# Attention scores of two heads in the two row halves of TensorE, in an order from a model of all engines

## The chip, the cores and the metric

The kernel runs on one core of a Trainium2 chip. The metric is the device time in microseconds, the median over runs. Differences of 2% (53 us here) count as faster or slower.

## What is computed

Two transformer layers on x of shape (2, 2048, 256), with 16 heads of 16 columns each. Both feed-forward layers have weights reduced to sign and a scale. The parts around the change are the two attentions:

```python
# layer a: causal softmax, then times a decay table
att = jnp.einsum('bhqd,bhkd->bhqk', q, k) * (1.0 / math.sqrt(hd))
att = jnp.where(causal, att, -jnp.inf)
att = jax.nn.softmax(att, axis=-1)
att = att * decay_weight_matrix(T)
y = jnp.einsum('bhqk,bhkd->bhqd', att, v)
# layer b: the same without the decay, with biases on q, k, v
x = x + attention_a(layernorm(x)); x = x + ffn(layernorm(x))
x = x + layernorm_affine(attention_b(layernorm(x))); x = x + ffn(layernorm(x))
```

The decay falls to zero at a distance of about 512 positions, so of layer a only a band of keys is needed for y, while the softmax's maximum and sum need all keys.

## The kernel before

Six phases run one after the other, each with its own buffers: `setup`, `projections` (q, k and v of layer a), `attention` "att_a" (decayed), `dense` "mid", `attention` "att_b" (dense in the sense of no decay), `dense` "end". Only `attention`, the plan that orders it and a few constants of `setup` are touched.

**Operands.** q and k are kept as a high and a low part of an fp32r number. A head has 16 columns; its score is the sum of four products (high by high, high by low, and so on), laid under each other in 64 rows (`PAIRS * HD`). Rows 64 to 127 of `kop` hold ones, and row 64 (`MROW`) of `qop` holds the negated maximum of each query, so that one matmul of 128 rows gives score minus maximum. The rest of the rows in `qop` are zero. The padding is written by `pad` (L601) on VectorE and GpSimd.

**Loops.** The 2 × 16 heads are 8 groups of 4 heads (`GH`). In a group, queries come in 4 chunks of 512 (`c`), keys in 16 blocks of 128 (`kb`). The items of work are:

- M (L814 to L831): a matmul of 128 queries by up to 512 keys into one of 4 banks `pm`; VectorE reduces it to one maximum per query (L759, and L763 where the causal mask cuts it). 160 in a group.
- FX, FE, FM, FT: only in att_a, exponentials and sums of the pieces of keys beyond the band, on ScalarE (L724) in the same bank.
- MF, MC: the maxima of a chunk are joined, turned by VectorE (L799) and moved into row 64 of `qop` by 4 DMAs on SyncE's queue (L652).
- S (L833 to L847): a matmul of 128 keys by up to 512 queries into one of 3 banks `ps`; in att_a a second one of 128 columns (`mask_k`, L845) puts the causal mask on the diagonal block. ScalarE writes the exponential to `wt` (L718). 160 in a group of att_b, 112 in one of att_a.
- in att_a GpSimd multiplies by the decay (L688, 2 buffers `wd`); in att_b it cuts the diagonal block (L698).
- PO and PV (L859, L864, L873): four heads' weights times ones (sums) or values, in four strips of 32 columns of the array, into the one bank `po`. fp32 matmuls, two records each in the trace.
- O, SU: ScalarE copies `po` out, the sums are moved by DMA, inverted and stored.
- L: loads of the next group's q, k (L622, L624) and v (L632) on SyncE's queue.

**Order.** `attention_plan` (L456) writes one list of items by hand rules: two streams (M, and S with what follows it) are laid over each other by their TensorE cost, the M stream 0.38 (att_a) or 0.45 (att_b) of a group ahead (`LEAD`). Every engine runs through the same list and takes the items that concern it, with semaphore waits. TensorE thus executes its matmuls strictly in the order of the list.

## Time and profile before

| | |
|---|---|
| median of 2 runs | 2672.27 us (2669.0 to 2675.54) |
| the profiled execution | 2671.95 us, span on the core 2670.2 us |
| granted TensorE clock, mean | 0.951 |

The profile page gives busy time of each engine over the span; "busy" is the union of its instructions, so overlapping ones count once. PE is TensorE's matmuls, PEld its weight loads, DVE VectorE, ACT ScalarE, POOL GpSimd, SPq the DMA queue fed by SyncE. L12 is line 12 of the kernel. Stages were cut by the first and last instruction of their tiles: att_a from 147.3 to 1133 us, att_b from 1466 to 2408 us. A matmul's time in the timeline reaches from its start to its modelled last result; the spacing of starts is what it costs.

### The profile page before, as it was taken

The numbers are of one execution on the slowest core, as the hardware profiler recorded it, in microseconds if no ns is written. First come the engines' busy times: TensorE is split into PE (matmuls) and PEld (weight loads), VectorE is DVE, ScalarE is ACT, GpSimd is POOL, SyncE is SP. The second block draws the span as 40 slices with busy tenths as digits, with TensorE's granted clock in tenths as the row PEclk, the third lists the DMA queues.
The fourth block names the chain that finished last, engine by engine and source line by source line (L and its number), as shares of the span: only waits on it lengthen the run. The fifth ranks groups of instructions, "written<-read, shape, count | busy, mean of one in ns | idle before, by whom it ended". The sixth has DMA issues, their size and how long they took to land. (4 is left out here: it accounts for less than half of the span.)

```text
span 2670.2 us, 43926 instructions
## 1 busy us (share of the span) xinstructions
PE 2396.0 (90%) x13600; PEld 1367.6 (51%) x13600; DVE 1962.1 (73%) x4834; ACT 1499.8 (56%) x3293; POOL 1054.0 (39%) x1274
## 2 busy tenths in 40 slices
PE   4969999999999999859996899999999999992887
PEld 2544545555454545346764455555555555532666
DVE  5677888878888888337653988888888878833887
ACT  1218677776868777614331266666666666670233
POOL 0037778788787778813211301010010110103552
PEclk8969999999999999979998699999999999996999
DMA  4684243351615330053323644261542615004210
GB/s 150 255 145 59 37 55 51 45 73 18 85 26 66 46 50 10 10 164 115 130 98 123 88 65 62 30 85 30 66 61 30 85 26 70 10 9 140 77 50 32
DMA packets 158806, 188.69 MB, mean 71 GB/s; under 512 B 65520, under 2 KB 89584, under 8 KB 157808
## 3 DMA queue, kind: packets, MB, share of 16 engines
q1 hardware_dynamic: 153840, 175.91, 33.5%
q10 hardware_dynamic: 4736, 9.96, 1.9%
q8 instruction: 113, 1.85, 0.3%
q14 instruction: 117, 0.96, 0.2%
HBM read 114.37 MB, written 69.99 MB: 69 GB/s over the span
## 5 line engine op out<-in xcount | busy, mean ns | idle before, releaser
L688 POOL TENSOR_TENSOR att_a_wd<-att_a_wt,decay 128x256 f32<-128x256 f32 (+3 forms) x896 | 754.4, 872 | 208.5 <-PE att_a_po L864 120.5
L718 ACT ACTIVATE att_b_wt<-att_b_ps 128x512 f32<-128x512 f32 (+3 forms) x1280 | 592.3, 540 | 325.5 <-PE att_b_ps L842 323.7
L759 DVE TENSOR_REDUCE att_a_mpart<-att_a_pm 128x1 f32<-128x512 f32 x768 | 508.8, 686 | 115.9 <-PE att_a_pm L829 110.8
L759 DVE TENSOR_REDUCE att_b_mpart<-att_b_pm 128x1 f32<-128x512 f32 x768 | 503.5, 685 | 95.4 <-PE att_b_pm L829 93.7
L829 PE MATMUL att_a_pm<-att_a_kop,att_a_qop 128*128 128x512 f32 (+3 forms) x1280 | 510.8, 425 | 45.5 <-DMA att_a_kop<-qk 19.1
L718 ACT ACTIVATE att_a_wt<-att_a_ps 128x512 f32<-128x512 f32 (+3 forms) x896 | 433.0, 511 | 207.2 <-PE att_a_ps L845 145.0
L829 PE MATMUL att_b_pm<-att_b_kop,att_b_qop 128*128 128x512 f32 (+3 forms) x1280 | 486.7, 400 | 29.7 <-DMA att_b_kop<-qk 18.4
L842 PE MATMUL att_b_ps<-att_b_qop,att_b_kop 128*128 128x512 f32 (+3 forms) x1280 | 453.9, 384 | 13.7 <-DMA att_b_qop<-att_b_mrow 9.1
L698 POOL TENSOR_SCALAR_AFFINE_SELECT att_b_wt<-att_b_wt 128x512 f32<-128x512 f32 x128 | 81.4, 636 | 837.4 <-ACT att_b_wt L718 837.4
L829 PEld LDWEIGHTS att_a_pm<-att_a_kop,att_a_qop 128*128 128x128 f32 x1280 | 237.9, 193 | 307.2 <-DVE att_a_mpart L759 139.7
L829 PEld LDWEIGHTS att_b_pm<-att_b_kop,att_b_qop 128*128 128x128 f32 x1280 | 244.9, 194 | 245.9 <-DVE att_b_mpart L759 119.3
L842 PE MATMUL att_a_ps<-att_a_qop,att_a_kop 128*128 128x512 f32 (+3 forms) x896 | 319.4, 366 | 0.7 <-ACT att_a_wt L718 0.7
L842 PEld LDWEIGHTS att_b_ps<-att_b_qop,att_b_kop 128*128 128x128 f32 x1280 | 236.9, 189 | 131.2 <-ACT att_b_wt L718 80.9
L873 PE MATMUL att_b_po<-att_b_wt,att_b_va 128*17 128x512 f32 (+3 forms) x2560 | 296.4, 535 | 1.1 <-POOL att_b_wt L698 1.0
L724 ACT ACTIVATE att_a_pm<-att_a_pm,att_a_mpart 128x512 f32<-128x512 f32 x384 | 258.1, 673 | 69.3 <-DVE att_a_mpart L759 66.9
L763 DVE CUSTOM_DVE_ANT_0 att_a_pm<-att_a_pm,late 128x384 f32<-128x384 f32 (+3 forms) x512 | 248.4, 496 | 48.7 <-PE att_a_pm L829 47.2
L763 DVE CUSTOM_DVE_ANT_0 att_b_pm<-att_b_pm,late 128x384 f32<-128x384 f32 (+3 forms) x512 | 248.0, 497 | 43.7 <-PE att_b_pm L829 43.4
L842 PEld LDWEIGHTS att_a_ps<-att_a_qop,att_a_kop 128*128 128x128 f32 x896 | 169.9, 190 | 66.7 <-ACT att_a_wt L718 52.0
L859 PE MATMUL att_a_po<-att_a_wt,ones_strip 128*32 128x512 f32 (+3 forms) x1792 | 198.0, 513 | 1.8 <-ACT att_a_y L738 1.6
L864 PE MATMUL att_a_po<-att_a_wd,att_a_va 128*16 128x256 f32 (+3 forms) x1792 | 164.8, 440 | 2.9 <-POOL att_a_wd L688 2.8
L1262 ACT ACTIVATE end_g<-end_ph,b,alpha 128x512 f32<-128x512 f32 x64 | 50.0, 782 | 124.9 <-PE end_ph L1197 112.9
L845 PE MATMUL att_a_ps<-mask_k,identr 128*128 128x128 f32 x512 | 118.8, 236 | 0.0
(167 smaller groups left out, 2512.1 us busy)
## 6 DMA issues: line engine op xcount, KB each, us to landing
att_a_kop<-qk SPq DMA_DIRECT2D x128, 128.0 KB, 7.0
att_b_kop<-qk SPq DMA_DIRECT2D x128, 128.0 KB, 6.0
att_a_qop<-qk SPq DMA_DIRECT2D x112, 128.0 KB, 6.6
att_b_qop<-qk SPq DMA_DIRECT2D x112, 128.0 KB, 6.6
qk<-qkv_a_qk_hi SPq DMA_DIRECT2D x8, 1024.0 KB, 4.1
qk<-qkv_a_qk_lo SPq DMA_DIRECT2D x8, 1024.0 KB, 6.0
y<-att_a_y SPq DMA_DIRECT2D x32, 256.0 KB, 2.2
qk<-mid_qk_hi SPq DMA_DIRECT2D x8, 1024.0 KB, 4.3
```

The costliest lines, as they stand in the source:

```text
L688: pool.tensor_tensor(wd[:, kq % 2, j, a:z], wt[:, kq % buffers, j, a:z], keep["decay"][:, u:u + z - a], ALU.mult).then_inc(w_decayed, 1)
L698: pool.affine_select(out=block, in_=block, compare_op=ALU.is_ge, fill=0.0, base=0, pattern=[[0, GH], [1, P]], channel_multiplier=-1).then_ ...
L718: act.activation(wt[:, kq % buffers, j, a:CH], pe_[:, n % EBANKS, 0:CH - a], ACT.Exp)\
L724: act.activation(pm[:, n % MBANKS, :], pm[:, n % MBANKS, :], ACT.Exp, bias=mpart[:, c, piece, u:u + 1], accum_out=fsum[:, c, piece, u:u + ...
L759: dve.tensor_reduce(mpart[:, c, piece, u:u + 1], pm[:, n % MBANKS, 0:w], AX.X, ALU.max, negate=True).then_inc(m_reduced, 1)
L763: dve.tensor_tensor_reduce(out=pm[:, n % MBANKS, 0:w], in0=pm[:, n % MBANKS, 0:w], in1=keep["late"][:, CH - w:CH], scale=-1.0, scalar=-2 * ...
L829: mm = pe.matmul(pm[:, n % MBANKS, 0:w], qop[:, par, c, j, qb * P:(qb + 1) * P], kop[:, par, j, piece * CH:piece * CH + w], start=True, st ...
L842: mm = pe.matmul(pe_[:, n % EBANKS, 0:CH - a], kop[:, par, j, kb * P:(kb + 1) * P], qop[:, par, c, j, a:CH], start=True, stop=not diagonal)
L845: mm = pe.matmul(pe_[:, n % EBANKS, 0:P], keep["identr"][:, :], keep["mask_k"][:, :], start=False, stop=True)
L859: pe.matmul(po[STRIP * j:STRIP * (j + 1), a:CH], keep["ones_strip"][:, :], wt[:, kq % buffers, j, a:CH], start=first, stop=False)
L864: mm = pe.matmul(po[STRIP * j:STRIP * j + VW, a:z], va[:, par, kb, j, :], wd[:, kq % 2, j, a:z], start=False, stop=last)
L873: mm = pe.matmul(po[STRIP * j:STRIP * j + VW, a:CH], va[:, par, kb, j, :], wt[:, kq % buffers, j, a:CH], start=first, stop=last)
```

## The change

- **Halves.** Rows 0 to 63 of `kop`, `qop` hold two heads of a group, rows 64 to 127 the other two (`HALF`, `half(h)`). M and S are matmuls of 64 rows in one half of the array. `pad` goes away.
- **X.** The maximum is subtracted by a matmul of its own on the same bank: `ones_row` (64 rows of ones, 128 columns) by `mx`, a new buffer whose first row in each half holds the maxima and whose other rows are zero. In att_a the mask of a diagonal block is now two matmuls of 64 columns (`tri`). S opens the bank; X, a new item, masks, subtracts and signals ScalarE. At most two scores are open.
- **Row moves and loads.** MC needs 8 DMAs instead of 4 (two halves), a load of q or k is two DMAs of half the size, and L comes in 16 pieces of a group, one row quarter of a chunk each. The copy of zeros over row 64 goes away.
- **Buffers.** `wd` has 3 buffers, the parts of the maxima and sums (`mpart`, `fsum`, `frow`) two sets by parity of the group.
- **Order.** `attention_plan` is now a class that simulates TensorE's halves, VectorE, ScalarE, GpSimd and the moves with fixed costs, and at each step takes the item with the earliest start (a key with small corrections). M may be up to 0.75 of a group ahead. M items are taken from two streams, one for each half. The last group goes through its chunks from the last to the first.

```diff
+SEEN, ROW, SUMS = 290.0, 6000.0, 9000.0
+URGENT, WEIGH, APART, AHEAD = 60.0, 0.0, 6, 0.75
+PATIENCE = (500.0, 0.0, -600.0, -2000.0)
+HEADS = (0, 2, 1, 3)
...
+def sequence(g):
+
+    return range(NC) if g < GROUPS - 1 else range(NC - 1, -1, -1)
...
+    def run(self, a, start, columns):
+        self.issued = max(start, self.free[a], self.issued)
+        self.free[a] = self.issued + 20.0 + columns / 2.4
+        return self.free[a] + SEEN
...
+        self.dve = max(self.dve, end) + 100.0 + w / 0.96
...
+    def product(self, start, kind, v, columns):
+        g, c, kb = self.visits[v]
+        self.issued = start
+        self.free = [start + 180.0 + columns * 8 / 2.4 / 2] * 2
...
+        half = lambda a: max(self.free[a], self.issued)
+        both = max(self.free) + 90.0
+        if self.open:
+            a = HEADS[self.open[0] % GH] // (GH // 2)
+            yield half(a), half(a) - URGENT, self.subtract, ()
+        for a in range(2):
+            if self.used[a] == len(self.streams[a]) or self.used[a] - self.used[1 - a] >= APART:
+                continue
...
+        if self.scores < GH * len(self.visits) and len(self.open) < 2:
...
-        kop = sb("kop", [P, 2, GH, T], F32R)
-        qop = sb("qop", [P, 2, NC, GH, CH], F32R)
+        kop = sb("kop", [P, 2, GH // 2, T], F32R)
+        qop = sb("qop", [P, 2, NC, GH // 2, CH], F32R)
+        mx = sb("mx", [P, 2, NC, GH // 2, CH], F32R)
...
-        wd = sb("wd", [P, 2, GH, CH], F32) if decayed else None
+        wd = sb("wd", [P, WD, GH, CH], F32) if decayed else None
...
+                    for a in range(2):
+                        row = mx[HALF * a:HALF * a + 1, g % 2, c, :, :].bitcast(F32)
+                        row = row.rearrange("o j (t k i) -> o (j t) k i", t=TB, k=P // SQUARE)
+                        for k in range(P // SQUARE):
+                            units = slice(SQUARE * k + SQUARE // 2 * a, SQUARE * k + SQUARE // 2 * (a + 1), SPREAD)
+                            sp.dma_start(row[:, :, k, :], mrow[units, c, :].bitcast(F32)).then_inc(m_in[c], 16)
...
-                    mm = pe.matmul(pm[:, n % MBANKS, 0:w], qop[:, par, c, j, qb * P:(qb + 1) * P],
-                                   kop[:, par, j, piece * CH:piece * CH + w], start=True, stop=True)
+                    mm = pe.matmul(pm[:, n % MBANKS, 0:w], qop[rows, par, c, j, qb * P:(qb + 1) * P],
+                                   kop[rows, par, j, piece * CH:piece * CH + w], start=True, stop=True)
...
-                    mm = pe.matmul(pe_[:, n % EBANKS, 0:CH - a], kop[:, par, j, kb * P:(kb + 1) * P],
-                                   qop[:, par, c, j, a:CH], start=True, stop=not diagonal)
-                    if diagonal:
-                        mm = pe.matmul(pe_[:, n % EBANKS, 0:P], keep["identr"][:, :], keep["mask_k"][:, :],
-                                       start=False, stop=True)
...
+                    pe.matmul(pe_[:, n % EBANKS, 0:CH - a], kop[rows, par, j, kb * P:(kb + 1) * P],
+                              qop[rows, par, c, j, a:CH], start=True, stop=False)
+                if kind == "X":
+                    for i in range(2 if decayed and kb >= TB * c else 0):
+                        tri = keep["tri"][rows, (0, 1, 2, 0)[2 * (h // (GH // 2)) + i], :]
+                        pe.matmul(pe_[:, n % EBANKS, HALF * i:HALF * (i + 1)], tri, keep["identr"][rows, rows],
+                                  start=False, stop=False)
+                    mm = pe.matmul(pe_[:, n % EBANKS, 0:CH - a], keep["ones_row"][rows, :], mx[rows, par, c, j, a:CH],
+                                   start=False, stop=True)
                     mm.then_inc(e_scores, 1)
```

## Rows read from the trace of the kernel before

**Rows 1.** The page: span, and busy time by engine.
```profile
span 2670.2 us, 43926 instructions
PE 2396.0 (90%) x13600; PEld 1367.6 (51%) x13600; DVE 1962.1 (73%) x4834; ACT 1499.8 (56%) x3293; POOL 1054.0 (39%) x1274
```

**Rows 2.** Busy by stage: window, its length, engines, TensorE clock, DMA share, GB/s.
```profile
147.30:1133.00 985.70, 939.47 (x6272) 490.13 (x6272) 781.68 (x1982) 696.12 (x1713) 775.43 (x908) 0.98 0.35 49
1466.00:2408.00 942.00, 902.69 (x5120) 477.66 (x5120) 741.54 (x1894) 605.77 (x1313) 102.44 (x140) 0.97 0.37 51
```

**Rows 3.** Tile views (ns min/median/max, first to last start), then groups of the page.
```profile
L842 PE MATMUL att_a_ps<-att_a_qop,att_a_kop x896: 218/392/632, 194.0 to 1128.6; 128*128 128x512 f32 x103, 128*128 128x384 f32 x26, 128*128 128x256 f32 x26, 128*128 128x128 f32 x25
...
L842 PE MATMUL att_b_ps<-att_b_qop,att_b_kop x1280: 218/393/796, 1514.9 to 2404.1; 128*128 128x512 f32 x129, 128*128 128x256 f32 x19, 128*128 128x384 f32 x18, 128*128 128x128 f32 x17
...
L829 PE MATMUL att_b_pm<-att_b_kop,att_b_qop x1280: 218/395/797, 1476.6 to 2359.5; 128*128 128x512 f32 x128, 128*128 128x128 f32 x19, 128*128 128x256 f32 x18, 128*128 128x384 f32 x18
...
L688 POOL TENSOR_TENSOR att_a_wd<-att_a_wt,decay 128x256 f32<-128x256 f32 (+3 forms) x896 | 754.4, 872 | 208.5 <-PE att_a_po L864 120.5
L718 ACT ACTIVATE att_b_wt<-att_b_ps 128x512 f32<-128x512 f32 (+3 forms) x1280 | 592.3, 540 | 325.5 <-PE att_b_ps L842 323.7
...
L759 DVE TENSOR_REDUCE att_b_mpart<-att_b_pm 128x1 f32<-128x512 f32 x768 | 503.5, 685 | 95.4 <-PE att_b_pm L829 93.7
```

**Rows 4.** Timeline of PE in att_b: start us, us, what, count.
```profile
1806.82 0.41 PE L873 MATMUL att_b_po<-att_b_wt,att_b_va 128*17 128x128 f32 x8
1807.16 0.50 PE L842 MATMUL att_b_ps<-att_b_qop,att_b_kop 128*128 128x512 f32 x1
1807.49 0.40 PE L829 MATMUL att_b_pm<-att_b_kop,att_b_qop 128*128 128x512 f32 x1
...
1808.42 0.39 PE L829 MATMUL att_b_pm<-att_b_kop,att_b_qop 128*128 128x512 f32 x1
1808.65 0.40 PE L842 MATMUL att_b_ps<-att_b_qop,att_b_kop 128*128 128x512 f32 x1
1808.98 1.05 PE L873 MATMUL att_b_po<-att_b_wt,att_b_va 128*17 128x512 f32 x8
1809.96 0.56 PE L829 MATMUL att_b_pm<-att_b_kop,att_b_qop 128*128 128x512 f32 x2
```

**Rows 5.** Waits: who waited for whom, us in total, times, longest.
```profile
PEld att_a_pm L829 <- DVE att_a_mpart L759: 139.7, 225, 1.1
```

**Rows 6.** Timeline: fp32 matmuls over the whole array, then weight loads in att_b.
```profile
130.85 7.03 PE L417 MATMUL qkv_a_pqk<-qkv_a_xt,qkv_a_wqkv 128*128 128x512 f32 x16
...
1802.55 0.19 PEld L842 LDWEIGHTS att_b_ps<-att_b_qop,att_b_kop 128*128 128x128 f32 x1
1802.66 0.19 PEld L829 LDWEIGHTS att_b_pm<-att_b_kop,att_b_qop 128*128 128x128 f32 x1
1802.98 0.13 PEld L873 LDWEIGHTS att_b_po<-att_b_wt,att_b_va 128*17 128x17 f32 x8
```

**Rows 7.** Timeline of DVE in att_b, two maxima one after the other.
```profile
1941.19 0.69 DVE L759 TENSOR_REDUCE att_b_mpart<-att_b_pm 128x1 f32<-128x512 f32 x1
1941.79 0.69 DVE L763 CUSTOM_DVE_ANT_0 att_b_pm<-att_b_pm,late 128x512 f32<-128x512 f32 x1
```

**Rows 8.** First maximum of att_a; SyncE's queue there and in att_b.
```profile
157.75 6.19 PE L829 MATMUL att_a_pm<-att_a_kop,att_a_qop 128*128 128x128 f32 x16 [16.42 <-DMA att_a_kop<-qk]
...
159.16 14.10 SPq L632 DMA_DIRECT2D att_a_va<-v  x2
173.36 14.32 SPq L652 DMA_DIRECT2D att_a_qop<-att_a_mrow  x8
...
188.34 0.43 SPq L624 DMA_DIRECT2D att_a_qop<-qk  x1
188.81 0.43 SPq L622 DMA_DIRECT2D att_a_kop<-qk  x1
...
1801.28 2.49 SPq L652 DMA_DIRECT2D att_b_qop<-att_b_mrow  x4
```

More of the change, by code:

```diff
@@ L502, in spaced @@
-def spaced(m, decayed):
-    out, late = [], []
-    def follow(*items):
-        late.extend([delay, cost, item] for delay, cost, item in items)
-    for cost, item in m:
-        out.append((cost, item))
-        for x in late:
-            x[0] -= 1
-        out += [(x[1], x[2]) for x in late if x[0] == 0]
-        late[:] = [x for x in late if x[0] > 0]
-        if item[0] == "M" and item[6] in far(item[3], decayed):
-            follow((1, 0.0, ("FX", *item[1:])))
-        if item[0] == "MF":
-            g, c = item[1:]
-            follow((3, 0.0, ("MC", g, c)))
-            if far(c, decayed):
-                follow((8, 0.0, ("FE", g, c)), (11, 0.0, ("FM", g, c)), (14, 0.0, ("FT", g, c)))
-    return out + [(200.0, x[2]) for x in sorted(late, key=lambda x: x[0])]
+def sequence(g):
+    return range(NC) if g < GROUPS - 1 else range(NC - 1, -1, -1)
@@ L601, in pad, with counts @@
-        def pad(eng, t, par, padded):
-            for c in range(NC):
-                part = t[MROW:P, par, :, c * CH:(c + 1) * CH] if t is kop else t[MROW:P, par, c, :, :]
-                eng.memset(part.bitcast(F32), 1.0 if t is kop else 0.0).then_inc(padded, 1)
+        QK_LOADS = 16 * 4 * PAIRS
+        M_DMAS = 16 * 2 * (P // SQUARE)
+        Y_DMAS, S_DMAS = 16, 16 * (P // SQUARE)
+        PLAN = attention_plan(decayed, MBANKS, EBANKS, buffers, WD)
+        def counts(kind):
+            seen, after = 0, {}
+            for item in PLAN:
+                if item[0] == kind:
+                    seen += 1
+                    after[item[1], item[3] if kind in ("M", "X", "FX", "PV") else item[2]] = seen
+            return after
@@ new lines, in done, with side, half, load @@
+        def done(g, c):
+            return place(g, c) + 1
+        def side(g, c):
+            return place(g, c) % 2
+        def half(h):
+            a = h // (GH // 2)
+            return slice(HALF * a, HALF * (a + 1)), h % (GH // 2)
+        def load(eng, g, c, r, k_too, q_too):
+            par, cols = g % 2, slice(c * CH, (c + 1) * CH)
+            for a in range(2):
+                part = slice(HALF * a + HD * r, HALF * a + HD * (r + 1))
+                heads = slice(GH // 2 * a, GH // 2 * (a + 1))
+                if k_too:
+                    eng.dma_start(kop[part, par, :, cols].bitcast(F32), qk_g[g][r % 2, 1, :, heads, cols])\
+                       .then_inc(qk_in[par][c], 16)
+                if q_too:
+                    eng.dma_start(qop[part, par, c, :, :].bitcast(F32), qk_g[g][r // 2, 0, :, heads, cols])\
+                       .then_inc(qk_in[par][c], 16)
@@ L813, in _ @@
             pe.sem_inc(pv_done, buffers)
+            begun = set()
             for item in PLAN:
@@ L827, in _ @@
-                    if FARS:
-                        pe.wait_ge(f_done, FAR_UNITS * g + far_left(n) + MBANKS)
-                    mm = pe.matmul(pm[:, n % MBANKS, 0:w], qop[:, par, c, j, qb * P:(qb + 1) * P],
-                                   kop[:, par, j, piece * CH:piece * CH + w], start=True, stop=True)
+                    _, _, n, c, qb, h, piece = item
+                    rows, j = half(h)
+                    for a in range(c + 1):
+                        if (g, a) not in begun:
+                            pe.wait_ge(qk_in[par][a], QK_LOADS * (g // 2 + 1))
+                            begun.add((g, a))
@@ L841, in _ @@
[L841 to L846 removed]
+                        pe.wait_ge(v_in[par], 16 * NC * (g // 2 + 1))
```

473 lines of the change are left out of this document (284 added, 189 removed).

## The prediction

> **What bounds the kernel now.** I read the page first: one execution, span 2670.2 us, TensorE (PE) busy 90% of it [rows 1]. A share over the whole span says little, so the next view was busy time by stage. Decayed attention takes 985.7 us and dense attention 942.0 us; everything else, 742.5 us, is untouched by the diff. In both attention stages PE is busy 95%, VectorE (DVE) 79%, and the TensorE clock is at 0.98 and 0.97 of its upper level, 2.4 GHz [rows 2]. So PE is the densest engine, but DVE follows closely (781.7 and 741.5 us), and in the decayed stage GpSimd (POOL) too, 775.4 us.
>
> Is PE really the bound? The tile views give pace: the scores for the weights (line 842) start at 194.0 and end at 1128.6 in the decayed stage, 1514.9 to 2404.1 in the dense one [rows 3]. That is 934.6/8 = 116.8 us and 889.2/8 = 111.2 us for each of 8 groups. The timeline of PE shows how a group fills up: 512-column matmuls start 0.23 us apart (1808.42, 1808.65), whichever operands they take; 512 columns at 2.4 GHz are 0.213. A set of four heads' weights times values (eight records, four 32-column strips side by side) occupies PE for 0.98 us with 512 columns and 0.34 with 128, and costs 0.10 more on entry (0.33 between 1808.65 and 1808.98) and 0.10 on leaving (1807.16 to 1807.49) [rows 4]. So a set costs 1.18, 0.97, 0.75 or 0.54 us for 512, 384, 256 or 128 columns (the middle two interpolated).
>
> Dense group: 40 sets (4, 8, 12 and 16 key blocks for the four chunks), 28 with 512 columns and 4 each of the rest, 33.0 + 9.0 = 42 us. The other 69 us go to 160 maxima matmuls and 160 score matmuls: 0.216 us each, about what columns plus spacing give. Decayed group: 28 sums sets (PO; 16 + 4 with 512 columns, 4 each of the rest, 32.6 us) and 28 value sets (7 of each width, 24.1 us), together 57 us; the remaining 60 us are 272 maxima and scores and 64 masks. With 4 us for the masks (0.06 each: 128 columns) a matmul comes to 0.206 us. PE's own work therefore fills the pace, and PE is the bound. The waits show the same from the other side: ACT waits 323.7 us for scores in the dense stage [rows 3]. PE's weight loads do wait 139.7 us for DVE's reductions in the decayed stage [rows 5], but these waits pass mostly beside a matmul that still runs: PE stays 95% busy.
>
> **The change, part by part.** *Halves.* A maxima matmul keeps its columns but uses 64 rows, so one of the other two heads can run in the other half. Per group 160 matmuls become 80 on each half. *Scores.* The maximum row no longer rides in the contraction (row 64); it is a second matmul (ones_row by mx) onto the same bank. So S becomes S + X: 320 matmuls in a dense group, 224 in a decayed one. *Masks.* Each of 64 masks becomes two of 64 columns, each with its own 128-column weight load.
>
> No row shows two row halves at once. The nearest are the column strips. In the projections the same fp32 kind over the whole array takes (7.03 - 0.59)/15 = 0.43 us per record of 512 columns [rows 6]; eight of them in a row would be 3.4 us, and a set's eight take 0.98 [rows 4], two rounds of four at once. Their eight weight loads lie within 0.13 us, while two full-width loads start 0.11 us apart [rows 6]. Strips overlap entirely, so I take full overlap of halves; no overlap stays as the other end. With full overlap, each half works off (160 + 320)/2 = 240 matmuls at 0.216 = 51.8 us; plus 42 us of sets = 94 us per dense group instead of 111. Decayed: 192 × 0.206 = 39.6, plus 64 masks per half at 0.12 (a 64-column matmul cannot hide a 0.11 us load [rows 6]) = 7.7, plus 57 = 104 us instead of 117.
>
> The Trainium skill (TensorE: Matmul & The Clock Gate, section "The mechanism") says that a weight load overlaps a running matmul only when its row group differs. The trace disagrees: full-height loads are hidden now, with 0.23 us between 512-column matmuls and 0.11 us for a load [rows 4, 6]. The measurement decides.
>
> *What is late next.* DVE: its 96 full reductions per group follow each other at 0.60 us when fed (1941.19, 1941.79), against 0.66 of busy time each [rows 7, 3], so 741.5/8 = 92.7 us fall by 96 × 0.06 to 87 per dense group; the decayed one, less the padding memsets (some 7 us of the stage), is (781.7 - 7)/8 - 6 = 91. POOL's decay products are 754.4/8 = 94 us per group [rows 3]. ACT is at 87 and 76 us [rows 2]. So PE's sums of 104 and 94 us still end last, but with the others within 10% and a fixed order I add 3 and 4 us: **pace 107 us (decayed) and 98 us (dense)**. Score banks: a bank was held for 0.40 (matmul) + 0.54 (exp [rows 3]); with X and one score in between it is 1.4 us, by three banks 0.47 us a unit, 75 us a dense group: below the pace.
>
> *Queues.* Each row move (MC) is 8 DMAs instead of 4 on SP: 4 took 2.49 us [rows 8], so 5 us, 32 times a stage; loads are 64 issues a group instead of about 36, 30 us of SP at 0.47 each. Behind them stand the sums (O) and the next rows. With about 66 of 100 us SP stays off the path except where a row is needed at once. Zeroing mx on POOL (8 memsets) is hidden behind the first loads: the first maximum waited 16.4 us for DMA [rows 8].
>
> *Start and end.* Now the scores of the first group start 46.7 (194.0) and 48.9 us (1514.9) into the stage, because the plan sets them back by 0.38 and 0.45 of a group. After, they need only the first row. But in the decayed stage SP's va loads block until 173.4 and the first eight row DMAs took 14.3 us [rows 8], so I take 184. They then use up chunks 0 to 2 (20 of 28 visits, 73 us at 103) by 257; the last chunk's maxima are then done (157.8 + 92 = 250). From 257: 7.29 groups × 107 = 780, plus 4 to the last store = 1041: stage 894 us, **-92**. Dense: group 0's maxima end at 1476.6 + 90 = 1567, its row lands 7 us later, 24 of 40 visits are through by then; 1574 + 7.4 × 98 + 4 = 2303: stage 837 us, **-105**. The turned order of the last group keeps the last visits (chunk 0) short; it is in the 4 us.
>
> Sum: 2671.95 (the profiled execution, 0.3 below the median of 2672.27) - 92 - 105 = 2475. The first group runs ahead while PE is still free, which the 7.29 and 7.4 groups count at full pace; I take 10 off: **2465 us**.
>
> **Rivals.**
> *A, the fixed order is off.* The plan costs DVE, ACT, POOL and DMA with constants (a row 6 us, sums 9 us) and PE takes its stream strictly in order; a maximum ordered before its bank is free holds the other half too. For it: loads waited 139.7 us for reductions under the old order already [rows 5], and 8 row DMAs took 14.3 us under load, more than twice the 6 assumed [rows 8]. Against it: rows are made up to 0.75 of a group ahead. With 5 and 8 us lost per group the pace is 112 and 106: 930 and 896 us, sum 2570.
> *B, the halves do not overlap.* Then the added X is paid in full: dense 480 × 0.216 + 42 = 146, decayed 384 × 0.206 + 128 × 0.12 + 57 = 151 us a group; stages 1215 and 1190 us, +477: about 3150, slower. It decides below an overlap of about two thirds: 103.7 us of serial work must shrink to 69. For it: no row shows halves at once, and both would write 128 PSUM partitions each at full rate, which strips don't. Against it: the strips.
> *C, loads show within a half.* If a half's next load can't be hidden, each of its 512-column matmuls takes 0.213 + 0.11 = 0.32 instead of 0.23: +22 us per dense group (116), +17 decayed (121); with 2 us of waits 118 and 123, so 985 and 1011 us: about 2740, slower. The spacing in rows 4 speaks against it. This is what the rule of the Trainium skill named above would do here.
> *D, the change does more.* If PE falls below DVE and POOL and the order is good, 100 and 91 us: 843 and 785, about 2372.
>
> **Chances.** Forecast 0.62, D 0.04, A 0.18, B 0.11, C 0.05. The range for 8 in 10 reaches from D (2370) to a bit above A (2600) and leaves out B, C and little else; the likeliest case alone is 2400 to 2530. Two per cent (about what a measurement of this kernel tells from no change) is 53 us, so faster means below 2619: forecast, D and four fifths of A, 0.80; same 0.04; slower B and C, 0.16.
>
> **What would show it.** In the profile after: matmuls of lines for M, S and X with 64 rows starting in pairs a few hundredths apart, with pairs 0.23 us apart at 512 columns (halves right), or 0.23 between any two (B), or 0.32 within a half (C). PE's weight loads should wait on DVE in the dense stage, DVE's busy share there should rise from 79% to about 88%, and first scores come 35 to 40 us into a stage. Pace 107 and 98 us per group. The prediction is wrong if the sets of four heads cost more to enter from half mode than 0.10 us each way (40 sets in a dense group, 56 in a decayed one), or if PE's queue stands still before a full bank while the other half is idle.

## The result: 2627.7 us, a gain of 1.75% where 8% was forecast

The changed kernel takes 2627.68 us (median; 2620.94 to 2634.41), the kernel before 2672.27. The ratio is 0.9825, 95% interval 0.9801 to 0.985: less than the 2% that count as faster, so by the rule stated at the top the two kernels are the same, an outcome to which the prediction gave 0.04. The profiled execution took 2634.41 us, 169 more than the 2465 forecast and above the top of the range. The page after, span and busy time by engine, against [rows 1]:

```profile
span 2632.7 us, 49993 instructions
PE 2354.9 (89%) x16288; PEld 1350.9 (51%) x16288; DVE 1933.3 (73%) x4826; ACT 1470.5 (56%) x3293; POOL 1025.8 (39%) x1269
```

TensorE (PE) is busy for 41 us less than before, with 2,688 more matmuls. The stages, in the same view as [rows 2] (window, length, PE, PEld, DVE, ACT, POOL, granted clock, DMA share, GB/s):

```profile
147.30:1141.00 993.70, 930.33 (x7680) 504.84 (x7680) 774.16 (x1976) 670.32 (x1713) 758.43 (x905) 0.95 0.20 49
1468.50:2381.00 912.50, 873.27 (x6400) 448.45 (x6400) 719.51 (x1888) 602.65 (x1313) 86.77 (x135) 0.96 0.22 53
```

For all kernels below a stage is measured from the first load of queries to the first load of the next phase. So measured, the decayed stage went from 992.4 to 993.7 us and the dense one from 947.7 to 912.1: all of the gain is in dense attention. The tile view of the scores, against [rows 3] (ns min, median, max; first to last start):

```profile
L995 PE MATMUL att_b_ps<-att_b_qop,att_b_kop x1280: 215/393/793, 1504.1 to 2368.7; 64*128 64x512 f32 x129, 64*128 64x256 f32 x19, 64*128 64x128 f32 x18, 64*128 64x384 f32 x17
```

The page's group of ACT's exponentials, also against [rows 3]:

```profile
L870 ACT ACTIVATE att_b_wt<-att_b_ps 128x512 f32<-128x512 f32 (+3 forms) x1280 | 588.7, 541 | 282.9 <-PE att_b_ps L1002 279.6
```

And the waits (total us, times, longest), the last line against [rows 5]:

```profile
ACT att_b_wt L870 <- PE att_b_ps L1002: 279.6, 320, 21.0
PEld att_b_ps L995 <- ACT att_b_wt L870: 188.5, 384, 0.9
PEld att_a_pm L982 <- DVE att_a_mpart L910: 141.7, 223, 6.5
```

Weight loads for scores now wait 188.5 us for ACT's exponentials (80.9 before), while ACT still waits 279.6 us for scores. When two engines wait for each other in turn, a chain that runs through both can set the pace, and not the sum of work of either. The one wait of 6.5 us in the last line is a different matter, and comes up below.

Do two heads run at once? PE's timeline in the dense stage (start, us, what, count; records of one line joined):

```profile
2289.71 0.51 PE L995 MATMUL att_b_ps<-att_b_qop,att_b_kop 64*128 64x512 f32 x2
2289.94 0.51 PE L1002 MATMUL att_b_ps<-att_b_mx,ones_row 64*128 64x512 f32 x2
2290.18 0.39 PE L982 MATMUL att_b_pm<-att_b_kop,att_b_qop 64*128 64x512 f32 x2
2290.41 0.39 PE L995 MATMUL att_b_ps<-att_b_qop,att_b_kop 64*128 64x512 f32 x1
2290.46 0.50 PE L982 MATMUL att_b_pm<-att_b_kop,att_b_qop 64*128 64x512 f32 x1
2290.64 0.39 PE L1002 MATMUL att_b_ps<-att_b_mx,ones_row 64*128 64x512 f32 x1
2290.97 1.05 PE L1030 MATMUL att_b_po<-att_b_wt,att_b_va 128*17 128x512 f32 x8
2291.95 0.62 PE L982 MATMUL att_b_pm<-att_b_kop,att_b_qop 64*128 64x384 f32 x3
```

They do: two matmuls of 512 columns together last 0.51 us, and the next pair starts 0.23 us after the first. The set of eight still starts 0.33 after the last matmul and lasts 0.98, as in [rows 4]. But the halves are not full. Two windows of the dense stage (columns as above) have PE busy throughout:

```profile
1749.00:1853.00 104.00, 103.82 (x799) 52.23 (x798) 90.65 (x237) 74.86 (x165) 10.27 (x17) 1.00 0.22 58
1853.00:1957.00 104.00, 103.63 (x802) 51.89 (x801) 90.48 (x237) 75.04 (x164) 9.93 (x17) 1.00 0.21 58
```

Yet from 1749 to 2061 us, the columns of all matmuls that are not in sets, at 2.4 GHz, sum to 262.3 us and cover 167.0 us of time: 1.57 halves at work on average, not 2.

### The profile page after: what moved, and what is told of

The parts are those of the page before. It is cut to its first block and busy times, and to the rows that moved or that the text cites. A ratio compares the mean times of both kernels' runs of the same rounds, so it can differ in the third digit from the quotient of the medians.

```text
span 2632.7 us, 49993 instructions
## 1 busy us (share of the span) xinstructions
PE 2354.9 (89%) x16288; PEld 1350.9 (51%) x16288; DVE 1933.3 (73%) x4826; ACT 1470.5 (56%) x3293; POOL 1025.8 (39%) x1269
## 5 line engine op out<-in xcount | busy, mean ns | idle before, releaser
L842 POOL TENSOR_TENSOR att_a_wd<-att_a_wt,decay 128x256 f32<-128x256 f32 (+3 forms) x896 | 753.0, 876 | 225.5 <-ACT att_a_wt L870 214.6
L870 ACT ACTIVATE att_b_wt<-att_b_ps 128x512 f32<-128x512 f32 (+3 forms) x1280 | 588.7, 541 | 282.9 <-PE att_b_ps L1002 279.6
L910 DVE TENSOR_REDUCE att_b_mpart<-att_b_pm 128x1 f32<-128x512 f32 x768 | 493.6, 683 | 69.3 <-PE att_b_pm L982 67.0
L995 PE MATMUL att_b_ps<-att_b_qop,att_b_kop 64*128 64x512 f32 (+3 forms) x1280 | 433.9, 410 | 14.9 <-DMA att_b_mx<-att_b_mrow 10.7
L982 PE MATMUL att_b_pm<-att_b_kop,att_b_qop 64*128 64x512 f32 (+3 forms) x1280 | 412.5, 422 | 22.1 <-DMA att_b_kop<-qk 19.2
L982 PE MATMUL att_a_pm<-att_a_kop,att_a_qop 64*128 64x512 f32 (+3 forms) x1280 | 358.2, 446 | 46.2 <-DMA att_a_kop<-qk 18.4
L1002 PE MATMUL att_b_ps<-att_b_mx,ones_row 64*128 64x512 f32 (+3 forms) x1280 | 386.4, 368 | 0.0
L995 PEld LDWEIGHTS att_b_ps<-att_b_qop,att_b_kop 64*128 64x128 f32 x1280 | 205.2, 187 | 216.5 <-ACT att_b_wt L870 188.5
L914 DVE CUSTOM_DVE_ANT_0 att_a_pm<-att_a_pm,late 128x128 f32<-128x128 f32 (+3 forms) x512 | 247.2, 500 | 90.4 <-PE att_a_pm L982 88.5
L995 PE MATMUL att_a_ps<-att_a_qop,att_a_kop 64*128 64x512 f32 (+3 forms) x896 | 281.9, 390 | 11.9 <-DMA att_a_mx<-att_a_mrow 11.9
L1002 PE MATMUL att_a_ps<-att_a_mx,ones_row 64*128 64x512 f32 (+3 forms) x896 | 286.6, 400 | 0.0
L982 PEld LDWEIGHTS att_b_pm<-att_b_kop,att_b_qop 64*128 64x128 f32 x1280 | 211.8, 191 | 141.0 <-DVE att_b_mpart L910 63.0
L914 DVE CUSTOM_DVE_ANT_0 att_b_pm<-att_b_pm,late 128x128 f32<-128x128 f32 (+3 forms) x512 | 245.3, 502 | 41.4 <-PE att_b_pm L982 40.3
L1002 PEld LDWEIGHTS att_b_ps<-att_b_mx,ones_row 64*128 64x128 f32 x1280 | 217.1, 189 | 9.9
```

Of the source, the lines that this page charges most:

```text
L842: pool.tensor_tensor(wd[:, v % WD, h, a:z], wt[:, v % buffers, h, a:z], keep["decay"][:, u:u + z - a], ALU.mult).then_inc(w_decayed, 1)
L870: act.activation(wt[:, v % buffers, h, a:CH], pe_[:, n % EBANKS, 0:CH - a], ACT.Exp)\
L910: dve.tensor_reduce(mpart[:, g % 2, c, piece, u:u + 1], pm[:, n % MBANKS, 0:w], AX.X, ALU.max, negate=True).then_inc(m_reduced, 1)
L914: dve.tensor_tensor_reduce(out=pm[:, n % MBANKS, 0:w], in0=pm[:, n % MBANKS, 0:w], in1=keep["late"][:, CH - w:CH], scale=-1.0, scalar=-2 * ...
L982: mm = pe.matmul(pm[:, n % MBANKS, 0:w], qop[rows, par, c, j, qb * P:(qb + 1) * P], kop[rows, par, j, piece * CH:piece * CH + w], start=Tr ...
L995: pe.matmul(pe_[:, n % EBANKS, 0:CH - a], kop[rows, par, j, kb * P:(kb + 1) * P], qop[rows, par, c, j, a:CH], start=True, stop=False)
```

## The experiments

"Pace" is the time of one of eight groups, from first exponential to first exponential of the next. Stages and paces are read from the one profiled execution of each kernel. The kernels that leave out part of the work, or do it on the wrong rows (one half, short reads, short maxima, the three with other banks or a plan told of short maxima, short X, no masks), were run once. The kernel before has 117 to 119 us (decayed) and 111 to 115 (dense). In the change the middle groups of the dense stage take 103 to 104, those of the decayed stage 109 to 113, or 121 and 123 where a stall falls in.

**Halves under the order of before.** `attention_plan` is replaced by the one of the kernel before, with X one score behind S.

```
-    return Plan(decayed, mbanks, ebanks, buffers, wd).make()
+    # old_plan: the hand-made order of before; X of a score follows the next S
+            out.append(("S", g, scores, c, kb, HEADS[j]))
+            if pending: out.append(pending.pop(0))
+            pending.append(("X", g, scores, c, kb, HEADS[j]))
```

> The halves, the second matmul X and everything else of the change, but items in the hand-made order of the kernel before (heads 0, 2, 1, 3; X one score behind S; last group forward). Tells the order apart from the halves. If the simulated order brings what was gained in the dense stage, this kernel is slower than the kernel before: the added X costs, and its order was never made for alternating halves: 2700 to 2800 us. If the halves bring it by themselves, it comes out at 2630 or below.

Measured: 2840.3 us, ratio 1.0619 (1.0601 to 1.0636); stages 1028.8 and 1078.4, dense pace 127. So halves without the new order are a loss, larger than the 2700 to 2800 expected.

**The order without the halves.** Full-height matmuls of before with the row in the contraction, ordered by the simulation, the last group forward.

```
     def candidates(self):
-        for a in range(2):
+        for a in range(1):
     def subtract(self, start):
-        end = self.run(HEADS[k] // (GH // 2), start, CH - a + 2 * diagonal * (HALF + 48))
+        end = self.run(0, start, CH - a + diagonal * P)
-        self.items.append(("X", g, n, c, kb, HEADS[k]))
+        self.items.append(("S", g, n % (GH * (len(self.visits) // GROUPS)), c, kb, k))
```

> The order alone: the full-height matmuls of the kernel before (maximum in row 64, one mask matmul, no X), in an order made by the change's simulation, told that the array is one; last group forward, parts of maxima and sums in two sets. The kernel with halves in the hand-made order took 2840 us, so the order is worth 212 us to the halves; what are the halves worth to the order? Theory P (the score stream is held by the sets of four heads, by exponentials and by banks, and not by the array's columns, so the halves bring little): 2590 to 2650, about the changed kernel's 2628 or below, paces 111 to 114 and 104 to 106 us. Rival (TensorE's columns still count, the halves do save): 2660 to 2700, paces near 118 and 112.

Measured: 2631.61 us, ratio 0.9836 (0.9817 to 0.9855); stages 971.7 and 928.3; pace 113 to 115 and 108. Its stages (window view):

```profile
145.00:1117.00 972.00, 921.55 (x6272) 500.43 (x6272) 772.17 (x1984) 676.70 (x1713) 771.84 (x908) 0.97 0.36 50
1444.00:2372.00 928.00, 885.63 (x5120) 475.79 (x5120) 735.84 (x1895) 607.30 (x1313) 101.94 (x141) 0.97 0.36 52
```

TensorE's instructions are those of [rows 2] in number (6272 and 5120), and the stages, measured alike, are 21 and 19 us shorter (992.4 and 947.7 before). The dense pace of 108 is above the 104 to 106 expected.

**The last group forward**, with the halves, which makes the comparison exact.

```
-    return range(NC) if g < GROUPS - 1 else range(NC - 1, -1, -1)
+    return range(NC)
```

> Only the last group's chunks go forward again, as the other groups'. In the changed kernel the decayed stage shows 134 us for group 6 and 95 for group 7, against 109 to 113 for the groups in the middle. Theory R (the turned order makes the scores of group 7 wait for 40% of its maxima first): the decayed stage loses 10 to 20 us, the dense one 0 to 5, total 2610 to 2620. Rival (the turned order shortens the end, as it is meant to): 5 to 15 us slower, 2635 or above.

Measured: 2619.93 us, ratio 0.9789 (0.9773 to 0.9805); stages 983.9 and 908.7. The stages are 10 and 3 us shorter than in the change, but the intervals of the two kernels overlap. Of the 10 us, 9 are one group that took 121 us in the change, with a stall of DVE in it, and 113 here without. The last two decayed groups took 134 + 95 us turned and 113 + 114 forward, the dense ones 103.5 + 101.9 and 103.1 + 98.3: the turned order gains nothing, and costs some 3 to 4 us a stage in these executions. Against the order alone, the halves are worth 20 us in the dense stage, lose 12 in the decayed one (where three stalls of DVE, 7.8, 4.4 and 2.3 us, fall in), and are worth 12 us in all.

**Both halves of the work in one half of the array**: all M, S and X in rows 0 to 63.

```
-            return slice(HALF * a, HALF * (a + 1)), h % (GH // 2)
+            rows, j = slice(0, HALF), h % (GH // 2)
```

> All M, S and X matmuls use rows 0 to 63 (the output uses the first two heads of each group for all four); nothing else is changed. Tells how much the overlap of the halves gives in this order. If the halves overlap on the chip: every 512-column matmul costs 0.23 us by itself, paces 145 to 155 us, total above 3100. Rival (the array takes matmuls of two halves one after the other anyway): the same 2630.

Measured: 4181.19 us; stages 1383.6 and 2068.6. Two windows of it (columns as above):

```profile
500.00:1500.00 1000.00, 997.30 (x6159) 604.76 (x6156) 617.57 (x1545) 562.31 (x1381) 613.16 (x723) 0.88 0.12 32
2000.00:3000.00 1000.00, 999.96 (x3134) 582.81 (x3126) 421.07 (x978) 329.23 (x630) 38.69 (x61) 0.50 0.08 21
```

The clock, which no theory had in it, was at 0.50 (1.2 GHz) through the dense window though PE was busy throughout, so the dense pace of 253 us gives no price of the overlap at 2.4 GHz. In the decayed window the clock was mostly up, and four groups took 136 to 145 us, against 109 to 113 with both halves and 151 in rival B. With the pairs in the timeline above this puts B out.

**Short reads by DVE and ACT.** Their reads of maxima and scores are cut to 64 columns; PE's work stays.

```
-  dve.tensor_reduce(mpart[...], pm[:, n % MBANKS, 0:w], ...)
+  dve.tensor_reduce(mpart[...], pm[:, n % MBANKS, 0:64], ...)
-  act.activation(wt[:, v % buffers, h, a:CH], pe_[:, n % EBANKS, 0:CH - a], ACT.Exp)
+  act.activation(wt[:, v % buffers, h, a:a + 64], pe_[:, n % EBANKS, 0:64], ACT.Exp, scale=0.0)
```

> The reads of the score banks are cut: VectorE's maxima and ScalarE's exponentials take 64 columns of each bank instead of up to 512 (the output leaves out most of the maxima and of the weights); TensorE's and GpSimd's work and the order stay. Theory B (TensorE's order stands still because banks are not yet read): the dense pace falls from 104 us per group to 92 to 96, and TensorE's starts follow from its own work alone. Theory H (the halves themselves do not overlap fully on the chip): the pace stays at 102 to 104.

Measured: 2552.75 us; dense stage 864.0, pace 97 to 100 (one of 103); decayed 958.5, with eight DVE operations of up to 9.7 us in it. A window of the dense stage (columns as above):

```profile
1700.00:1900.00 200.00, 199.99 (x1643) 106.31 (x1637) 80.43 (x481) 72.45 (x336) 21.53 (x34) 1.00 0.23 62
```

This lies between the two theories. With DVE and ACT busy for 40% and 36% of the time, the dense pace falls by 5 to 6 us, to the 98 us that the forecast had, and PE never stands. So banks that are read for their full length cost the change 5 to 6 us a group, and about 98 us is what PE's matmuls take in this order without that. The order was made for full-length reads; one made for short ones wasn't tried.

**Short maxima.** Now PE's own maxima are 64 columns too, and the exponentials of scores full.

```
-                    w = CH if piece < c else P * (qb + 1)
+                    w = 64
```

> The work on maxima is cut to 64 columns on TensorE, VectorE and ScalarE (the output leaves out most maxima, and the weights are all one); scores, exponentials in full length, sets and the order stay. Theory P (the score stream alone sets the pace): paces hardly fall, dense 98 to 104 us, decayed 107 to 112. Rival (TensorE's sum of columns sets the pace): with 160 x 0.09 us less work per half and group, 88 to 92 and 98 to 102.

Measured: 2572.43 us; dense stage 896.1, pace 100 to 101 (one of 102.5). With 28% of the columns outside the sets gone (59,392 of 208,896 a group), the dense group is 3 us shorter. So in the dense stage the stream of scores sets most of the pace by itself. The change shows the same in its last group, where no maxima are left (window view):

```profile
2312.00:2350.00 38.00, 36.96 (x247) 16.55 (x244) 0.48 (x2) 29.61 (x64) 3.19 (x5) 1.00 0.03 9
```

64 exponentials in 38 us are 95 us a group, with DVE idle. That is on the high side, since the scores here are a little wider than a group's (462 columns on average against 435).

The decayed stage took 950.0 us and answers differently. Its groups at the full clock, in the change and then here:

```profile
549.00:662.00 113.00, 111.89 (x969) 61.12 (x968) 95.05 (x247) 83.42 (x216) 94.56 (x114) 1.00 0.20 54
```

```profile
760.00:859.00 99.00, 98.53 (x964) 53.38 (x960) 38.25 (x247) 65.56 (x214) 93.28 (x113) 1.00 0.23 61
```

All of GpSimd's products are still there, and three groups take 99 to 100 us. So GpSimd doesn't hold the 109 to 113 us of the change, and work on maxima, on PE, DVE and ACT together, is worth 10 to 14 us of a decayed group.

**A fourth score bank.** Short maxima with the split of the banks turned, under the order made for full-length maxima:

```
-        MBANKS, EBANKS = 4, 3
+        MBANKS, EBANKS = 3, 4
```

> As the run with short maxima (64 columns on all engines, weights all one), with 3 banks for maxima and 4 for scores instead of 4 and 3. Theory P's reason: after a set of four heads ScalarE runs dry, since only three scores can be waiting. Then a fourth bank lowers the dense pace from 101 to 86 to 93 us. Rival (the score stream is held by something else, as the exponentials a set must wait for): 97 to 101.

Measured: 2769.63 us, dense pace 109. The clock that the plan keeps while it orders gives 111 us for full-length maxima through three banks, and PE takes that order whatever the maxima are. So nothing follows on the score banks. The next two kernels tell the plan that maxima are short, and differ in the split of seven banks alone: the first keeps 4, 3.

```
     def maximum(self, a, start):
-        w = CH if piece < c else P * (qb + 1)
+        w = 64
-        MBANKS, EBANKS = 4, 3
+        MBANKS, EBANKS = 3, 4
```

> The short maxima again (64 columns in the matmul, its reduction and ACT's far exponentials; the rest of the maxima's columns is left out), three score banks and four maxima banks as in the change, but now the plan that orders the work is told that they are short. In the run before, its order was made for full-length maxima. Theory T (the chain of the scores through three banks sets the dense pace): although a dense group has some 20 us less of work for each half of the array, the pace stays at 98 to 101 us; the plan's own clock says 99.0. Theory E (TensorE's and VectorE's throughput set it, and the short maxima gained nothing only because the order wasn't made for them): dense pace 86 to 92 us. Time 2540 to 2590 by T, 2470 to 2510 by E.

> The same short maxima with a plan that is told of them, but four score banks and three maxima banks. Theory T: a fourth bank lets the next score in while three others are with ACT, so the dense pace falls to 87 to 93 us (the plan's own clock says 87.4), against 98 to 101 with three banks. Theory B (a bank isn't what holds the chain; ACT's exponentials one after another, or the entry into the sets of four heads do): dense pace within 3 us of that with three banks. In the decayed stage GpSimd's products and the sums come in, and the plan's clock says 110 with four score banks against 103 with three, so nothing is told apart there.

Measured: 2509.85 us with three score banks, dense pace 101 to 102 (two groups of 106 and 109); 2530.99 with four, dense pace 92 to 95 (two groups of 99). The dense stages took 878.4 and 822.9 us, 7 us a group apart. The same 100 us of both, first three, then four banks:

```profile
1664.00:1764.00 100.00, 97.81 (x780) 48.84 (x772) 38.11 (x227) 72.95 (x161) 10.17 (x16) 0.98 0.22 56
```

```profile
1664.00:1764.00 100.00, 97.08 (x854) 51.30 (x852) 37.11 (x254) 79.23 (x176) 10.15 (x16) 0.97 0.23 61
```

PE is "97% busy" in both, yet does 780 matmuls in the one and 854 in the other. By its pace theory T held in the dense stage: with short maxima the score banks set it. But the time with three banks, 2509.85 us, is theory E's, because the decayed stage fell to 900.8 us, with three groups of 99 to 102: the dense stage hardly feels the maxima, the decayed one does. With four banks the decayed stage took 974.6 us (pace 111 to 115, forecast 110). The plan's own clock had said that it would be slower; its trace also has a DVE addition of 6.1 to 6.6 us in each of six groups and 319 us at 1.2 GHz.

**The maximum row on 64 columns**: X is cut.

```
-  mm = pe.matmul(pe_[:, n % EBANKS, 0:CH - a], keep["ones_row"][rows, :], mx[rows, par, c, j, a:CH],
+  mm = pe.matmul(pe_[:, n % EBANKS, 0:64], keep["ones_row"][rows, :], mx[rows, par, c, j, a:a + 64],
```

> The matmul that subtracts the maxima takes 64 columns instead of up to 512 (the maxima are subtracted for 64 queries of a chunk only). Gives the price of X, which the full-height kernel doesn't have. If X is hidden beside the other half: dense pace 104 to 101 to 103. If it lies in the score stream's own chain (bank, S, X, exponential): 0.15 to 0.2 us per pair of heads, 93 to 98.

Measured: 2624.55 us; dense stage 881.4, pace 96 to 99 (two of 101 and 103); the decayed stage got longer, 1013.3, with 245 us at 1.2 GHz (106 in the change) and two stalls. X costs 6 us per dense group, so it is not hidden beside the other half.

**No masks.**

```
-                    for i in range(2 if decayed and kb >= TB * c else 0):
+                    for i in range(0):
```

> The changed kernel without its 128 mask matmuls per decayed group (future keys stay in, so the output is not causal in layer a). In the forecast they cost 7.7 us a group by 0.12 us each and half. If so: decayed pace 113 to 104 to 107. Rival (the decayed pace is held by the score stream's waits, in which the masks hide): 110 to 113. The dense stage keeps 912.

Measured: 2592.74 us; decayed stage 948.6, pace 108 to 110 against 113 in most groups: up to 5 us per group, between the two theories; dense stage unchanged, 912.1.

**The long stall in the decayed stage.** The change's timeline, GpSimd's row and DVE's and PE's (in brackets: idle before, and what ended it):

```profile
409.98 12.83 POOL L842 TENSOR_TENSOR att_a_wd<-att_a_wt,decay 128x512 f32<-128x512 f32 x11
...
415.01 7.84 DVE L959 TENSOR_TENSOR att_a_scol<-att_a_scol,att_a_frow 128x32 f32<-128x32 f32 x1
...
422.89 0.35 DVE L961 RECIPROCAL att_a_inverse<-att_a_scol 128x32 f32<-128x32 f32 x1
...
423.54 0.79 PE L982 MATMUL att_a_pm<-att_a_kop,att_a_qop 64*128 64x512 f32 x1 [6.04 <-DVE att_a_mpart L914]
```

An addition of 32 columns (0.30 us as a rule) ends when eleven products on GpSimd end, at 422.81; PE then stands for 6 us. It happens twice (7.84 and 7.92 us), and the clock then falls to 1.2 GHz for 13.7 and 6.8 us. Two kernels, with one of the two added statements each: the addition on GpSimd, or as a sum over one input on DVE.

```
-  dve.tensor_tensor(scol[:, i, :], scol[:, i, :], frow[:, g % 2, n, :], ALU.add)
+  pool.tensor_tensor(scol[:, i, :], scol[:, i, :], frow[:, g % 2, n, :], ALU.add)
+  dve.tensor_reduce(ssum[:, i, :], both_sums[:, i:k + 1:k - i, :].rearrange("p n u -> p u n"),
+                    AX.X, ALU.add)
```

> The addition of the far sums (two SBUF inputs, 128x32) is done by GpSimd instead of VectorE, 16 times in the decayed stage. In the changed kernel two of these additions took 7.8 and 7.9 us on VectorE while GpSimd ran decay products back to back, PE stood still for 6 us each time and its clock fell to 1.2 GHz for 13.7 and 6.8 us after. Theory L (VectorE was kept out by GpSimd's stream): both stalls and both clock drops are gone, the decayed stage is 15 to 25 us shorter, 2605 to 2615. Rival (the stall is a wait of another kind and moves along with the addition): no change beyond 5 us, or GpSimd stands still in its place.

Measured: 2660.36 us, ratio 0.9952 (0.9935 to 0.9968); decayed stage 1014.7. The two stalls are gone, but the time is 45 us above the 2605 to 2615 expected: GpSimd, in order, waits for the sums' DMA (11.4 us by the profile), and PE stands 2.2 to 2.8 us in six groups.

> The same addition of far sums as in the run that moved it to GpSimd, but it stays on VectorE as a reduction over two rows of one buffer, which has one input instead of two. Moving it to GpSimd took both long stalls away but cost 5 us a group, since decay products then waited behind it for the sums' DMA. Theory L (a two-input operation from SBUF is kept out while GpSimd streams, a one-input reduction is not): both 7.8 us additions are gone, decayed stage 10 to 20 us below 994, total 2608 to 2620. Rival (any SBUF operation of VectorE is kept out): an addition of several us is still there.

Measured: 2622.73 us, ratio 0.9798 (0.9772 to 0.9824); decayed stage 978.0. The tile view of the new sum shows none that waits (ns, shortest, median and longest):

```profile
L962 DVE TENSOR_REDUCE att_a_ssum<-att_a_both_sums x16: 209/216/224, 287.9 to 1084.1; 128x32 f32<-128x64 f32 x16
```

The decayed stage is 16 us shorter than in the change, in the two groups that had the stalls (123 and 121 us, now 112 and 113.5). The intervals of the two kernels' times overlap, so this rests on the two traces.

**The best of both**: decayed stage at full height, dense stage in halves, both in the simulated order, last group forward.

```
-        attention(nc, "att_a", True, keep, scratch)
+        attention_full(nc, "att_a", True, keep, scratch)
```

> The best parts together: the decayed stage with full-height matmuls in the simulated order (971.7 us as measured), the dense stage with halves (908.7 us with the last group forward), the rest 728 us. If the stages keep their times: 2600 to 2615, ratio 0.971 to 0.976 to the kernel before and 0.5 to 1% below the changed kernel. Rival (the stage times measured in one execution each were luck): 2620 to 2630.

Measured: 2613.02 us, ratio 0.9758 (0.9744 to 0.9773); stages 972.3 and 908.8. It beats the kernel before and the change. With the one-input sum as well:

> The best kernel so far (decayed stage at full height and dense stage in halves, both in the simulated order, last group forward; 2613) with the far sums in the decayed stage added by a one-input reduction on VectorE in place of the two-input addition. Theory L (a two-input operation of VectorE can be kept out of the memory while GpSimd runs one product after another): its decayed stage, 972 us, had few of the long additions, so 3 to 10 us less, 2603 to 2610. Rival: no change within 2 us, since the additions of this order fell beside pauses of GpSimd anyway.

Measured: 2610.3 us, ratio 0.975 (0.9728 to 0.9772); decayed stage 968.3. Its page:

```profile
span 2608.2 us, 46859 instructions
PE 2346.4 (90%) x14880; PEld 1348.1 (52%) x14880; DVE 1924.7 (74%) x4830; ACT 1476.4 (57%) x3293; POOL 1037.3 (40%) x1275
```

The stage is 4 us shorter, but the two intervals overlap, so this last step isn't shown by the times. Nor do the traces show the sums as its cause: none of them took over 0.64 us in the kernel before this one. What went away are four of five long operations (2.5 us) of another kind, the two-input subtractions into `ffactor`, which the edit doesn't touch; why they went stays open.

## Why the prediction failed, step by step

**Where the 169 us lie.** Measured alike, the forecast for the stages was 992.4 - 92 = 900 and 947.7 - 105 = 843. They took 993.7 and 912.1: 93 and 70 us more. The remaining 7 are the 10 us taken off, less 3 in the rest of the kernel. In each stage:

| us | forecast | measured | missed by |
|---|---|---|---|
| decayed: group 0's weights done at | 288 | 316 | 28 |
| decayed: the other seven groups | 7 x 107 = 749 | 808 | 59 |
| dense: group 0's weights done at | 1613 | 1642 | 29 |
| dense: the other seven groups | 7 x 98 = 686 | 727 | 41 |

In the decayed stage the remaining 6 us are its earlier start (2 us) and its end (4 us).

**"PE is the bound" was half right, and "score banks: below the pace" was the step that failed.** The prediction said that a bank is held for 1.4 us, and three banks make that 0.47 us a score, 75 us a dense group. The holding time was right: from a score's start to the end of its exponential the trace has 1.34 us on average (482 scores, 1749 to 2061 us). What was left out is the time until the next score can enter that bank, 0.60 us more. The array goes to a set of four heads after every fourth score, and nothing enters while its 1.2 us run: 0.34 of the 0.60 us falls into sets, the rest behind other matmuls. A bank turns round in 1.94 us; by three 0.65, times 160 = 103.5 us, which is the dense pace. With four banks and short maxima a bank turns in 2.34 us: 0.585 x 160 = 93.6, measured 92 to 95. The prediction's sum added the sets to PE's work but left them out of the chain. The turn times 160 over the banks must give the pace in any kernel, so this product alone proves nothing. What shows that the chain holds the pace is that 28% fewer columns bring 3 us, that scores alone take up to 95 us, and that the fourth bank brings 7 to 9. That is shown with short maxima. With full-length ones a fourth score bank leaves three for the maxima, 111 us by the plan's own clock, and that wasn't tried. For the change itself short reads give the size: the 5 to 6 us a group that full-length reads cost are about the 41 us that the seven dense groups missed. That run doesn't tell the score banks from those of the maxima.

The prediction named two signs of being wrong. A dearer entry into the sets did not come (0.33 us, as before). PE's queue at a full bank did: 188.5 us of weight loads waiting for ACT.

**The halves.** "Pairs start together, 0.23 us apart" came true. The prediction's sum took both halves as full: 480 matmuls in 51.8 us, 17 less than the 69 it had for before, and 42 us of sets. From start to start, a dense group now has 58.1 us outside the sets and 45.8 at them; before it was 65.5 and 46.2. (The time at a set is counted from the start of the last matmul before it, so some 8 us a group are that matmul's own, and the figure can't be held against the 42.) So the saving outside the sets is 7 us, not 17, and the sets cost the same as before. Of the 8 us of dense pace gained, the order alone gives about 4 (112 to 108) and the halves 4 (to 104).

**Decayed stage.** Forecast 107 us, measured 115 on average over the last seven groups. Masks cost up to 5 us a group, not 7.7. The two stalls of DVE make 16 of the 59 us, the turned last group some 3. With both set aside, the halves and the full height come to nearly the same here: 109 to 114 us a group against 113 to 115, but a slower first group (135 against 129). What holds the remaining 109 to 113 us stays open. It isn't GpSimd (753 us of products, 94 a group), since with the same products and short maxima groups took 99 to 102. Nor is it the chain of scores alone, since that run left the scores as they were. The chain has the masks and a second set in it and meets the maxima and the far exponentials on PE, DVE and ACT; no run tells these apart.

The groups of the page that carry the stage's other engines, against those of [rows 3]:

```profile
L842 POOL TENSOR_TENSOR att_a_wd<-att_a_wt,decay 128x256 f32<-128x256 f32 (+3 forms) x896 | 753.0, 876 | 225.5 <-ACT att_a_wt L870 214.6
...
L910 DVE TENSOR_REDUCE att_b_mpart<-att_b_pm 128x1 f32<-128x512 f32 x768 | 493.6, 683 | 69.3 <-PE att_b_pm L982 67.0
```

Neither changed much: GpSimd's products went from 754.4 to 753.0 us, DVE's reductions in the dense stage from 503.5 to 493.6. The forecast took both as the next limits, but neither stage came down to them.

**What was left out: DVE and GpSimd hold each other up.** I weighed both as throughputs. The Trainium skill (SBUF — State Buffer, section "SBUF: two separate sides") says that a DVE operation with two inputs in SBUF and a GpSimd operation that reads SBUF exclude each other for a whole instruction. It bears on line 959 and was not in the prediction. The trace agrees in kind, and goes further in size: 7.84 us is over six of GpSimd's products (12.83/11 = 1.17 us each), not one. The same page, in "Who interferes with whom", has it that a reduction never contends; by that rule the one-input sum should not wait, and the trace agrees: 0.22 us at most in sixteen.

**Start of a stage.** First scores at 184 was right (180.4), and 38 us into the dense stage as forecast. But "they then use up chunks 0 to 2 by 257" was wrong. The early start bought nothing: before, group 0's weights were done at 194.0 + 117 = 311 and 1514.9 + 111 = 1626, now at 316 and 1642. PE first waits for the row, strictly in order:

```profile
161.03 8.27 SPq L778 DMA_DIRECT2D att_a_va<-v  x4
169.42 9.93 SPq L808 DMA_DIRECT2D att_a_mx<-att_a_mrow  x8
...
180.42 0.79 PE L995 MATMUL att_a_ps<-att_a_qop,att_a_kop 64*128 64x512 f32 x2 [6.35 <-DMA att_a_mx<-att_a_mrow]
```

(8.84 us in the dense stage.) Then the plan runs maxima ahead by up to 0.75 of a group in place of scores. That work is paid back only at the end, where scores alone take up to 95 us a group anyway, so a lead in maxima is worth little when the scores' chain is the bound. The clock adds to it: within group 0, 30 and 31 us ran at 1.2 GHz, against 3 and 0 before. The plan's own clock, which knows no fall of TensorE's, already has 126 and 131 us for the two groups 0, against 134 and 137 measured, so most of what they took beyond a middle group lies in the order. How the 28 us split between the row, the lead and the clock stays open.

**The rivals.** B and C are out: pairs start together, and the next pair 0.23 us later. A, the fixed order, had the sign of the miss but not its cause: its pace for the dense stage, 106, is near 104, but the plan's own clock says 103 for a dense group and 112 for a decayed one. So the order did what it was made to; a simulation of all engines had the bound that a sum by engine hadn't. A's 8 DMAs for a row and its 6 us showed up at the start of the stages alone. PE's weight loads were to wait for DVE in the dense stage: those for maxima wait 63.0 us for line 910, less than the 188.5 us for ACT. DVE's busy share there was to rise to 88% and stayed at 79% (719.5 of 912.5 us): nothing had come down far enough to press on DVE.

## What to carry to other kernels

When a tile passes through a ring of PSUM banks, compute the ring's turn, from entry to the next entry into the same bank, with every exclusive block of work on the array that falls into it, and compare that with each engine's sum. A test in one stage doesn't carry over to another: short maxima left the dense pace nearly as it was and took 10 us or more off a decayed group. A busy share near 97% says nothing on how much of the array works: count matmuls per 100 us. And before work is packed into halves of the array, see whether the order alone, at full height, brings most of the gain; here it brought 1.6% of the 2.1% that order and halves bring together.

## What the runs showed of the hardware that was not expected

- With one half of the array alone the granted clock stayed down: with all M, S and X in rows 0 to 63 PE was busy for 999.96 of 1000 us and the clock stood at 1.2 GHz, 0.50 of its upper level (one execution). With a share of other work (the masks and twice the sets, decayed stage) it was 0.88. In the change's dense stage, with both halves at work from 1749 to 1957 us, it was 1.00.
- A two-input operation of DVE on 32 columns took up to 7.9 us beside back-to-back products on GpSimd in the change, 18.2 us with short maxima, 32.2 without masks and 33.4 with X cut; the same sum over one input took 0.22.
- Two halves with 64 rows each run side by side at 0.23 us per pair of 512 columns, though each writes all 128 partitions of its own PSUM bank.
